# ScalarE's Sqrt and VectorE's reciprocal in place of GpSimd's power in the last six layer-norm tiles

## The reference, cut to what matters

```python
h = jnp.einsum('bsh,bhk->bsk', hidden_states, Wd) + bd[:, None, :]
h = jax.nn.gelu(h, approximate=False)
h = jnp.einsum('bsk,bkh->bsh', h, Wu) + bu[:, None, :]
h = residual + h
mean = jnp.mean(h, axis=-1, keepdims=True)
var = jnp.mean(jnp.square(h - mean), axis=-1, keepdims=True)
h = (h - mean) * jax.lax.rsqrt(var + LN_EPS)      # LN_EPS = 1e-05
return h * g[:, None, :] + b[:, None, :]
```

## Time and profile before

| | |
|---|---|
| median of 3 runs | 1032.73 us (1032.29 to 1033.24) |
| the profiled execution's own time | 1032.2 us |
| its span in the trace | 1030.4 us |
| busy: PE, PEld | 1023.4 us (99%), 858.0 us (83%) |
| busy: DVE, ACT, POOL | 795.0 us (77%), 524.8 us (51%), 26.5 us (3%) |
| granted TensorE clock | 0.999 of full speed |

### The profile page before, as it was taken

How to read it: one execution, slowest core, us unless ns; L and a number is a source line. 1 busy time by engine, 2 the same in 40 slices (tenths; PEclk the granted TensorE clock), 3 DMA queues, 4 the chain that set the end, 5 groups by cost and what they waited for, 6 DMA issues and landing times.

```text
span 1030.4 us, 13832 instructions
## 1 busy us (share of the span) xinstructions
PE 1023.4 (99%) x4834; PEld 858.0 (83%) x4834; DVE 795.0 (77%) x1364; ACT 524.8 (51%) x954; POOL 26.5 (3%) x42
## 2 busy tenths in 40 slices
PE   9999999999999999999999999999999999999997
PEld 8899888888888888888889888888888888888886
DVE  5657857767598898887966896677668889887798
ACT  4337864444265443433565587454435644434357
POOL 0000000000000021000000000000000001200001
PEclk9999999999999999999999999999999999999999
DMA  9351311210143272621643312312004322423142
GB/s 209 61 205 39 102 42 49 74 41 21 62 157 118 93 201 86 166 80 54 239 118 109 116 62 82 123 42 82 21 21 163 143 85 100 162 101 107 42 164 82
DMA packets 108558, 103.71 MB, mean 101 GB/s; under 512 B 54254, under 2 KB 89418, under 8 KB 104650
## 3 DMA queue, kind: packets, MB, share of 16 engines
q1 hardware_dynamic: 108400, 102.81, 30.9%
q10 hardware_dynamic: 90, 0.02, 0.0%
HBM read 79.74 MB, written 20.97 MB: 98 GB/s over the span
## 4 chain that ended last, share of the span: by engine, by line
PE 96%; DVE 2%; ACT 1%; issue 0%; DVEq 0%; ACTq 0%
PE bank L231 31%; PE bank L232 31%; PE bank L233 31%; PE bank L270 1%; PE bank L259 1%; DVE z_last L1315 0%; DVE z_last L1326 0%; PE bank L473 0%; PE bank L246 0%; ACT gel L857 0%; DVE xp2l L1043 0%; DVE xp3l L1043 0%; ACT e3h L601 0%; ACT h33h L856 0%; ACT h32h L856 0%
## 5 line engine op out<-in xcount | busy, mean ns | idle before, releaser
L693 ACT ACTIVATE sbc<-sbc,bias 128x512 f32<-128x512 f32 x112 | 80.5, 724 | 234.1 <-DVE sbc L1134 170.0
L231 PE MATMUL bank<-hid_hi,w_lo 128*128 128x512 f32 x512 | 199.7, 390 | 0.0
L233 PE MATMUL bank<-hid_lo,w_hi 128*128 128x512 f32 x512 | 199.3, 389 | 0.0
L232 PE MATMUL bank<-hid_hi,w_hi 128*128 128x512 f32 x512 | 199.2, 389 | 0.0
L1159 DVE TENSOR_TENSOR acc<-bank,acc 128x512 f32<-128x512 f32 x224 | 153.7, 686 | 51.4 <-PE bank L233 51.0
L231 PE MATMUL bank<-ta_hi,w_lo 128*128 128x512 f32 x448 | 174.5, 390 | 0.0
L232 PE MATMUL bank<-ta_hi,w_hi 128*128 128x512 f32 x448 | 174.3, 389 | 0.0
L233 PE MATMUL bank<-ta_lo,w_hi 128*128 128x512 f32 x448 | 174.3, 389 | 0.0
L1134 DVE TENSOR_TENSOR sbc<-bank,sbc 128x512 f32<-128x512 f32 x144 | 97.9, 686 | 41.3 <-PE bank L233 40.9
L1043 DVE TENSOR_TENSOR w_lo<-w_raw,w_hi 128x256 fp32r<-128x256 f32 (+1 forms) x176 | 99.4, 594 | 36.8 <-ACT w_hi L601 36.7
L601 ACT ACTIVATE sbc<-bank 128x512 f32<-128x512 f32 x112 | 66.2, 593 | 114.3 <-PE bank L233 112.4
(11 more groups left out here) (223 smaller groups left out, 1537.8 us busy)
## 6 DMA issues: line engine op xcount, KB each, us to landing
w_raw<-in_L_cond_mW SPq DMA_DIRECT2D x48, 512.0 KB, 3.4
w_raw<-in_L_cond_cW SPq DMA_DIRECT2D x32, 512.0 KB, 4.3
pre_d<-sbc SPq DMA_DIRECT2D x10, 1024.0 KB, 3.9
sbc<-pre_d SPq DMA_DIRECT2D x10, 1024.0 KB, 7.5
x_blk<-in_x SPq DMA_DIRECT2D x64, 64.0 KB, 2.3
e_raw<-in_L_cond_W_down SPq DMA_DIRECT2D x8, 512.0 KB, 4.6
e_raw<-in_L_cond_W_up SPq DMA_DIRECT2D x8, 512.0 KB, 4.1
proj_hi<-aw_hi SPq DMA_DIRECT2D x2, 1024.0 KB, 10.1
```

Source lines behind the costliest of these rows:

```text
L231: nc.tensor.matmul(dst, w_l, a_h, start=start, stop=False, **kw)
L232: nc.tensor.matmul(dst, w_h, a_h, start=False, stop=False, **kw)
L233: return nc.tensor.matmul(dst, w_h, a_l, start=False, stop=stop, **kw)
L693: nc.scalar.activation(dst, dst, ACT.Gelu, **kw).then_inc(g_done[key], 1)
```

## The change

In the last six tiles the reciprocal root of the variance is made otherwise. ScalarE, right behind each tile's Square pass, takes `std = sqrt(ssq / 512 + eps)` (128x1, with `eps` as a bias held in SBUF), and VectorE takes the reciprocal of `std`. VectorE's epsilon instruction and GpSimd's power of those six tiles are gone. VectorE's order in a tile becomes: centred tile, reciprocal, output. In front of the statistics ScalarE runs a 1-element Sqrt (`warm`). VectorE fills `eps` once in the prologue. Waits are written out so that the centring waits for both sums. Besides, a branch for untransposed attention probabilities is taken out of the program's text; `MOVED` held all four pairs, so it never gave an instruction.

```diff
@@ act_expert_last
             act_up_bias(act, 2 * bb + 1)
+            nc.scalar.activation(warm[:, :], eps[:, :], ACT.Sqrt)
             act_stats(act)
@@ act_stats
                 nc.scalar.activation(sjunk[:, c % 5, 1, :], bank, ACT.Square, bias=nmean[:, col],
                                      accum_out=ssq[:, col]).then_inc(ssq_done, 1)
+                act.wait_ge(ssq_done, c + 1)
+                nc.scalar.activation(std[:, col], ssq[:, col], ACT.Sqrt, scale=1.0 / V, bias=eps[:, 0:1])\
+                    .then_inc(std_done, 1)
@@ dve_rstd_last
-        def dve_eps_last(dve, pp, t):
+        def dve_rstd_last(dve, pp, t):
             col = slice(TT * pp + t, TT * pp + t + 1)
-            dve.wait_ge(ssq_done, A_NO[(pp, t)] + 1)
-            nc.vector.tensor_scalar(veps[:, t:t + 1], ssq[:, col], 1.0 / V, LN_EPS, ALU.mult, ALU.add).then_inc(ve_done, 1)
+            dve.wait_ge(std_done, A_NO[(pp, t)] + 1)
+            nc.vector.reciprocal(rstd[:, t:t + 1], std[:, col]).then_inc(rstd_done, 1)
@@ dve_norm_last
             def finish(pp, t):
-                dve_eps_last(dve, pp, t)
+                dve.wait_ge(nmean_done, A_NO[(pp, t)] + 1)
+                dve.wait_ge(ssq_done, A_NO[(pp, t)] + 1)
                 dve_cent_last(dve, pp, t)
+                dve_rstd_last(dve, pp, t)
                 dve_out_last(dve, pp, t)
...
-            dve_eps_last(dve, 1, 3)
+            dve.wait_ge(ssq_done, A_NO[(1, 3)] + 1)
             dve_cent_last(dve, 1, 3)
+            dve_rstd_last(dve, 1, 3)
             dve_out_last(dve, 1, 3, LEFT)
             dve_out_last(dve, 1, 3, RIGHT)
@@ dve_prologue
+            nc.vector.memset(eps[:, :], LN_EPS).then_inc(consts, 1)
@@ pool_program
-            pool_norm(pool, 2 * NBAT - 2, (halves[0],) + tuple(singles[t] for _, t in A_STAT))
+            pool_norm(pool, 2 * NBAT - 2, halves[:1])
```

More of the change, by code:

```diff
@@ L98, in build @@
         warm = sb("warm", [P, 1])
+        eps = sb("eps", [P, 1])
+        std = sb("std", [P, 2 * TT])
         ta_hi = at("ta_hi", X0, [P, 7, 2, TB], F32R)
@@ L182, in build @@
         stored = [sem(f"stored{s}") for s in range(2)]
-        wtr_mm, fold_mm, bias_mm, v_mm, s_mm, pT_mm, down_mm, up_mm, l2_mm = (sem(n) for n in (
-            "wtr_mm", "fold_mm", "bias_mm", "v_mm", "s_mm", "pT_mm", "down_mm", "up_mm",
-            "l2_mm"))
+        wtr_mm, fold_mm, bias_mm, v_mm, s_mm, down_mm, up_mm, l2_mm = (sem(n) for n in (
+            "wtr_mm", "fold_mm", "bias_mm", "v_mm", "s_mm", "down_mm", "up_mm", "l2_mm"))
         y_mm, pv_mm, x_h, ao_done = ([sem(f"{n}{k}") for k in range(KT)] for n in ("y_mm", "pv_mm", "x_h", "ao_done"))
@@ L208, in build @@
             "max_done", "nmax_done", "rinv_done", "probs_done"))
-        nmean_done, ssq_done, half_done = (sem(n) for n in ("nmean_done", "ssq_done", "half_done"))
+        nmean_done, ssq_done, std_done, half_done = (sem(n) for n in ("nmean_done", "ssq_done", "std_done", "half_done"))
         st_done, ag_done, ve_done, rstd_done, z_cent = (sem(n) for n in (
             "st_done", "ag_done", "ve_done", "rstd_done", "z_cent"))
-        MOVED = (0, 1, 2, 3)
-        moved_up_to = lambda n: sum(1 for m in MOVED if m <= n)
         phase_of = lambda i: i // NQ
@@ L361, in pe_values @@
             for t in range(TT):
[L362 to L365, removed]
                 pe.wait_ge(exp_done, 4 * n + t + 1)
@@ L371, in pe_values @@
                 last.then_inc(v_mm, 1)
[L373 to L385, removed]
         def pe_attend(pe, n):
@@ L769, in act_probs_T @@
             for b in range(SEQ):
[L770 to L775, removed]
+                act.wait_ge(raw_in[i], 256 * (n // 2 + 1))
+                act_copy(by_key(pT_hi[i], b), moved(i, b)).then_inc(pT_h, 1)
         def act_ao(act, n):
@@ L1246, in dve_probs_T @@
                 dve.wait_ge(pT_h, 2 * n + b + 1)
[L1247 to L1250, removed]
+                sub(by_key(pT_lo[i], b), moved(i, b), by_key(pT_hi[i], b)).then_inc(pT_l, 1)
         def dve_blocks_T(dve, n):
@@ L1341, in dve_norm_last @@
             dve.wait_ge(ln_in[1], 64 * NBAT)
[L1342 to L1346, removed]
-            dve_eps_last(dve, 1, 3)
+            for t in range(TT - 1):
+                finish(1, t)
+            dve.wait_ge(ssq_done, A_NO[(1, 3)] + 1)
             dve_cent_last(dve, 1, 3)
+            dve_rstd_last(dve, 1, 3)
             dve_out_last(dve, 1, 3, LEFT)
@@ L1679, in pool_program @@
             halves = [slice(2 * h, 2 * h + 2) for h in range(2)]
-            singles = [slice(t, t + 1) for t in range(TT)]
             for b in range(NBAT):
@@ L1717, in move_probs @@
             i = n % 2
-            sp.wait_ge(blk_done, 2 * moved_up_to(n))
+            sp.wait_ge(blk_done, 2 * (n + 1))
             grid = lambda tile, quarter: tile[32 * quarter:32 * quarter + 32, :].rearrange("p (x c f) -> p x c f", c=4, f=32)
@@ L1820, in sync_program @@
                 sp.dma_start(proj_lo[:, slot, :], aw_lo[slot][:, :].bitcast(F32)).then_inc(proj_out, 16)
-            for n in MOVED:
-                if n < 2:
-                    move_probs(sp, n)
+            for n in range(2):
+                move_probs(sp, n)
             sync_mlp(sp, 0)
```

## The result

Over 18 runs each, the changed kernel takes 1034.55 us in the median (1033.92 to 1036.1) and the kernel before 1032.72 us (1031.97 to 1033.28): +1.83 us, a ratio of 1.0018 with a 95% interval of 1.0012 to 1.0025. Forecast were 1034.5 us and a range of 1033.5 to 1035.5. The direction is clear of the noise. The size lies just inside the 0.2% that the prediction took for the bound of no change, and the interval reaches across that bound (0.12% to 0.25%), so on which side of it the change lies is not settled.

The account below looks back on a forecast made before the run. TensorE bounds 96% of the span; in the last us VectorE and ScalarE run level. First Identity 1.52 us late, Sqrts net 0.36, output 0.89 behind the sum instead of 0.97: +1.8 on 1032.73 gives 1034.5 us, range 1033.5 to 1035.5.

Parts of the forecast that it names:

- Two chains within 0.06 us: Last tile: ScalarE's sum and VectorE arrive within 0.06 us; delaying the sum further delays the end by nearly the same.
- Load and `warm`, 1.52 us: ScalarE, between bias additions and first statistics: table load and `warm` lack cover, so the first Identity is 1.52 us late.
- A tile in 1.73 us: ScalarE, last six tiles: with the Sqrt, one tile takes 1.73 us instead of 1.50.
- Last sum 1.88 us late: ScalarE's last Square sum: out at 1028.11 instead of 1026.23 us, 1.52 from load and `warm`, 0.36 from Sqrts less idle time.
- Output 0.89 us behind the sum in place of 0.97: VectorE, last tile: output starts 0.89 us after the sum, was 0.97; epsilon gone and reciprocal added nearly cancel.
- Sum +1.8: Start of the last output on VectorE: 1029.00 instead of 1027.20 us, so the whole kernel is 1.8 us slower.
- A: Rival, before the first Identity: the switch costs a second empty stretch of 1.28 us, +3.1 us in all; chance 0.10.
- C: Rival, at the bias additions: the load runs hidden beside them and only the Sqrts count, +0.3 us; chance 0.05.
- B: Rival, ScalarE's six tiles: Sqrts cost more, 1.85 us a tile, +2.4 us in all; chance 0.18.
- D: Rival, last tiles: a gain from dropping GpSimd's hop and VectorE's epsilon, at most -0.1 us; chance 0.05 with any other gain.
- no backlog: VectorE, last six tiles: 1.53 us of work a tile against ScalarE's 1.73, so VectorE waits for ScalarE.
- The rule against the row: Table switch on ScalarE: trace rows say 1.28 us, the skill page some 2.66 with a drain; the prediction trusted the rows.

Follow-up runs that it names:

- its move: Changed kernel with the 1-element Sqrt and its table load moved ahead of the eight bias additions: tail +1.73 us, median +1.43 us against the kernel before.
- the three loads: Changed kernel with three 1-element instructions (Sqrt, Gelu, Sqrt), each with a table load, instead of one: tail +4.70 us, median +4.00 us against the kernel before.
- additions on GpSimd, with and without the change: Eight bias additions of pair 3 moved from ScalarE to GpSimd: changed kernel tail 15.71 us, median 1034.63; kernel before 16.06 us, 1034.83.
- the shared version: Changed kernel with pair 3's eight bias additions split, four on VectorE, two on GpSimd, two on ScalarE: median 1032.43 against 1032.53 us before, ratio 0.9997.
- e3h: Not a run: a buffer in the profile rows, written by ScalarE (ACT, L585), for which VectorE's e3l subtraction waited 0.15 us.

## Why the prediction was right, point by point

- **Two chains within 0.06 us.** Held, in the sense that every experiment that delayed ScalarE's sums delayed the end, and the one that gave ScalarE cover ended where the kernel before does. But "nearly the same" holds for the whole change only. With the load alone the last sum is 0.17 us later (1026.84 - 1013.85 = 12.99 behind `h33l`, 12.82 before) and the end 1.21: there the first sum decides, not the last.
- **Load and `warm`, 1.52 us.** From 0.10 us ahead of the end of the additions to 1.42 behind it: 1.52. The first Square, whose row needs no correction, gives the same: 1017.15 - 1013.41 = 3.74 us behind `h33l` before, 1019.64 - 1014.38 = 5.26 now. The rows of earlier loads gave it exactly, and "a load has no cover in a queue without idle time" is borne out by its move (+1.73) and by the cover (-0.03, with the work moved to VectorE in it).
- **A tile in 1.73 us.** 1.71. The Sqrt takes 0.29 to 0.30 us, and its operand accounts for 0.09 of its spacing, as the estimate from `warm` and the two passes had it. The difference of 0.02 is the Identity: 0.58 us when it follows without a wait, 0.60 when TensorE releases it.
- **Last sum 1.88 us late.** Against `h33l` it is 1028.98 - 1014.38 = 14.60 now and 1026.23 - 1013.41 = 12.82 before: 1.78. The missing 0.1 is five times 0.02 us.
- **Output 0.89 us behind the sum in place of 0.97.** 1029.87 - 1028.98 = 0.89.
- **Sum +1.8.** The tail has +1.70, the medians +1.83; the two agree within the runs' scatter. That the median met the forecast to 0.05 us, closer than the tail met its own sum (0.1), is luck.
- **Rivals.** A is out by the three loads, C by the changed kernel's own row (the load starts behind the additions' end) and by the move of the load. B would have needed 1.79 us a tile. (Its sign, 0.35 us from a Sqrt's start to the next Identity, should have been 0.32 by its own terms; measured 0.20.) D is out for this kernel, whose last sum can't come before TensorE has the last tile. "No mechanism" was too strong, though: where VectorE bounds, its new order gained 0.35 us (additions on GpSimd, with and without the change).
- **What the prediction left unsaid.** It named VectorE as having no backlog, true for the whole change. It didn't see that without the Sqrts VectorE would become the bound, and its split of +1.88 into 1.52 for the load and 0.36 for the Sqrts is not what either costs by itself. On ScalarE the last sum is 0.17 us late without the Sqrts, 0.27 without the load, and 1.78 with both: ScalarE's idle time before the last three tiles takes up most of either one, and not both. At the end, taking the Sqrts away saves 0.77 us (1.70 - 0.93), not 0.36; taking the load away saves 1.51.

**The rule against the row.** The Trainium skill, "ScalarE: Activation LUTs", section "What ACT_TABLE_LOAD costs", adds to each switch a drain about as long as the load. No load behind other work that I read has one: those of the earlier trace rows, the one of the changed kernel (0.02 us behind the additions) and the three in a row, which are 1.50 us apart with an instruction of 0.20 between.

## What to carry to other kernels

Price a new function on ScalarE by its table load first, and look for the load's cover in the idle time of that engine's own queue, not in how small the function is. Idle time ahead of the place where the load stands covers it; with idle time behind it this engine catches up, but the engine that waited for the first result need not. Where two engines hand tiles to each other, count the chain of each from the first tile on: a delay of the first tile costs its full length on whichever of the two has no idle time between tiles. When work is moved to an idle engine, its duration there must come from rows taken beside what the other engines do at that time.

## What the hardware showed that was not expected

In the version with all additions on GpSimd, one addition of 128x256 took 0.92 us in the median of eight, but the first took 7.13 us (7.12 in the kernel before with its additions there), and 5.92 us in the shared version, all while VectorE went without a gap through subtractions with two operands in SBUF. VectorE in the first of them, over that stretch:

```profile
1002.57 2.49 DVE L1026 TENSOR_TENSOR xp3l<-acc,xp3h 128x512 fp32r<-128x512 f32 x4
1004.98 1.21 DVE L1026 TENSOR_TENSOR e0l<-e_raw,e0h 128x1024 fp32r<-128x1024 f32 x1
1006.12 2.35 DVE L1026 TENSOR_TENSOR e2l<-e_raw,e2h 128x1024 fp32r<-128x1024 f32 x2
1008.39 1.28 DVE L1026 TENSOR_TENSOR h32l<-gel,h32h 128x512 fp32r<-128x512 f32 x2
1009.82 2.40 DVE L1026 TENSOR_TENSOR e3l<-e_raw,e3h 128x1024 fp32r<-128x1024 f32 x2 [0.15 <-ACT e3h L585]
```

VectorE's first gap is at 1009.67 us, and GpSimd's addition ends 0.81 us behind it, at 1010.48. In the shared version the gap is at 1009.55 and the end at 1010.35. From the gap on, 0.8 us is about what an undisturbed addition takes, as if GpSimd had stood still until VectorE did. The Trainium skill, "SBUF — State Buffer", section "Who interferes with whom", says that a VectorE instruction with two SBUF inputs contends with a GpSimd one that reads SBUF, for a port that one of them holds for a whole instruction. That fits in kind, but here GpSimd waited through several of VectorE's instructions and not one. That it is this port and not another cause was not tested by itself.
